# Reordering one network block inside a woven single-core kernel: the u sigmoids before the z sigmoids, the scan one step earlier, an idle step between two top-1 units

## The reference: four blocks, of which the last two are touched

```python
def scan_block(hidden):                       # L1_attn
    x, z = split(hidden @ in_proj_w.T, 2)     # 256 + 256 features
    xc = silu(depthwise_conv4(x) + conv_b); u = xc
    dt_low, Bp, Cp = split(u @ x_proj_w.T, [8, 24])
    delta = softplus(dt_low @ dt_proj_w.T + 2 * dt_proj_b)
    # 16 states n: s = exp(delta * A[n]) * s + delta * Bp[n] * u ;  y += s * Cp[n]
    y = (y + u * D) * silu(z)
    return y @ out_proj_w.T
x = layernorm(x + scan_block(x))

def top1_block(x):                            # L1_ffn
    probs = softmax(x @ wg); idx = argmax(probs)
    # a token keeps its expert if fewer than T/8 earlier tokens chose it
    return gate * (x @ W[idx].T + b[idx])
x = layernorm(x + top1_block(x))
```

## Time and profile before

| | us |
|---|---|
| median of 3 runs | 1405.06 |
| lowest, highest | 1401.98, 1413.62 |
| the profiled execution's own time | 1411.83 |
| its span | 1410.0 |
| busy: PE, DVE, ACT, POOL | 905.6, 972.0, 594.3, 84.2 |
| mean granted TensorE clock (share of full) | 0.776 |

### The profile page before, as it was taken

One profiled execution on the slowest core, in us unless ns is written; L12 is line 12 of the kernel. 1 busy time (PEld: TensorE's weight loads), 2 busy tenths in 40 slices (PEclk: granted clock), 3 DMA queues, 4 the chain that ended last, 5 costly groups with the idle time before them and its releaser, 6 DMA issues.

```text
span 1410.0 us, 29222 instructions
## 1 busy us (share of the span) xinstructions
PE 905.6 (64%) x11808; PEld 545.3 (39%) x11808; DVE 972.0 (69%) x2254; ACT 594.3 (42%) x1299; POOL 84.2 (6%) x56
## 2 busy tenths in 40 slices
PE   4655656777567577788566677777657566472554
PEld 2444535444334244445234244444334244240122
DVE  5345543655689987656699987655689987335985
ACT  3333332466633332476633332466643331445320
POOL 0000000011000000020000000011000000030630
PEclk8556858599758889697768889698658789676897
DMA  4110110311223210311223210211223310302420
GB/s 143 31 40 10 33 39 10 66 35 39 67 68 87 69 31 18 67 36 37 67 68 87 69 31 12 57 42 39 66 63 86 76 31 10 68 1 62 112 67 8
DMA packets 84822, 72.19 MB, mean 51 GB/s; under 512 B 24528, under 2 KB 63440, under 8 KB 84496
## 3 DMA queue, kind: packets, MB, share of 16 engines
q1 hardware_dynamic: 84688, 70.34, 19.7%
HBM read 66.51 MB, written 3.80 MB: 50 GB/s over the span
## 4 chain that ended last, share of the span: by engine, by line
DVE 33%; PE 20%; ACT 12%; issue 11%; DMA 3%; SPq 2%; DVEq 0%; POOL 0%; ACTq 0%; POOLq 0%
DVE SG L1727 5%; PE bank L716 3%; PE bank L543 2%; DVE Y L1820 2%; DVE XP L1740 2%; PE bank L874 2%; DVE CV L1740 2%; SPq L480 2%; ACT QBD L1063 2%; DVE bank L1727 1%; PE bank L748 1%; PE bank L824 1%; ACT relu_s L1027 1%; DVE big L1715 1%; DVE big L1702 1%
## 5 line engine op out<-in xcount | busy, mean ns | idle before, releaser
L716 PE MATMUL bank<-onehot,tparts 128*32 128x256 bf16 x3840 | 134.8, 300 | 45.3 <-DVE onehot L1506 41.6
L716 PEld LDWEIGHTS bank<-onehot,tparts 128*32 128x32 bf16 x3840 | 108.7, 105 | 80.3 <-issue 70.7
L874 PE MATMUL bank<-XP,CO 128*128 128x512 f32 x128 | 86.1, 809 | 60.6 <-DVE XP L1738 33.2
L1727 DVE TENSOR_TENSOR_SCAN SG<-big 128x512 f32<-128x512 f32 x96 | 111.7, 1205 | 0.9
L1215 ACT ACTIVATE big<-DEL,Aneg 128x512 f32<-128x512 f32 x96 | 63.8, 715 | 102.5 <-DVE SG L1727 96.7
L1027 ACT ACTIVATE relu_s<-bank,nml 128x192 f32<-128x192 f32 (+1 forms) x128 | 52.9, 426 | 112.0 <-DVE nml L1472 112.0
L874 PE MATMUL bank<-CV,CO 128*128 128x512 f32 x128 | 77.3, 735 | 32.4 <-DVE CV L1740 20.4
L1467 DVE TENSOR_REDUCE ml<-bank 128x2 f32<-128x384 f32 (+1 forms) x64 | 33.8, 569 | 71.1 <-PE bank L651 38.5
L1506 DVE TENSOR_SCALAR onehot<-ib,CO 128x1024 bf16<-128x1024 f16 x160 | 69.5, 477 | 15.7 <-PE bank L716 14.5
L748 PE MATMUL bank<-GT,QBD 128*32 128x32 f32 x3072 | 56.6, 208 | 34.9 <-DVE G L1515 22.1
L543 PE MATMUL bank<-CO,relu_s 128*128 128x128 f32 (+2 forms) x256 | 45.8, 339 | 44.7 <-ACT relu_s L1027 44.7
(11 more groups left out here) (306 smaller groups left out, 2002.7 us busy)
## 6 DMA issues: line engine op xcount, KB each, us to landing
BC<-bc_rows SPq DMA_DIRECT2D x128, 256.0 KB, 4.4
ib<-idx_rows SPq DMA_DIRECT2D x64, 256.0 KB, 4.1
big<-comb_rows SPq DMA_DIRECT2D x8, 1024.0 KB, 10.0
rows_bounce<-RO SPq DMA_DIRECT2D x256, 8.5 KB
W<-w SPq DMA_DIRECT2D x1, 2818.0 KB, 14.8
RB<-rows_bounce SPq DMA_DIRECT2D x16, 136.0 KB, 2.1
X<-x SPq DMA_DIRECT2D x4, 256.0 KB, 3.0
out<-CV SPq DMA_DIRECT2D x4, 256.0 KB, 2.3
```

Source lines behind the costliest of these rows:

```text
L716: m = mm(bank[2 + c % 2][32 * bb:32 * bb + 32, 256 * kind:256 * kind + 256], tparts[:, kt, part, 32 * kind:32 * kind + 32], onehot[:, n % ...
L874: mm(bank[5 + j][:, :], ident, hC[(n - 1) % 2][:, j, :], start=(n == 1), stop=(n == DS)).then_inc(ysum.sem, ysum.up())
L1727: m = dve.tensor_tensor_scan(state, decay, dBu[:, n % 2, j, :], 0.0, ALU.mult, ALU.add)
```

## The change

ACT and DVE: the two u sigmoids (and `U` times the conv's result) come before the two z sigmoids (and `SZ` times z). PE, ACT, DVE, SP and POOL: `SCAN_IN_PHASES` is 9 instead of 10, so that everything from the u projection to the second top-1 unit lies one step earlier. `TOP1_PHASES` is 9 instead of 8, with an idle step between the second and the third top-1 unit, so the third and fourth unit and the last norm stay in their steps. No instruction is added, removed or resized.

```diff
@@ PE @@
                     mm(bank[3 + k][:, :], w("inp")[:, k * P:(k + 1) * P], XRT[:, :], start=True, stop=True).then_inc(xz_ps.sem, xz_ps.up())
-                for _ in range(3):
+                for _ in range(2):
                     yield
                 pe.wait_ge(u_ok.sem, u_ok.at(b, 2))
...
                 top1_out(1)
+                yield
                 yield
                 pe.wait_ge(e_used.sem, e_used.at(b, 2))
@@ ACT @@
                 yield
+                for j in range(2):
+                    act.wait_ge(cv_ok.sem, cv_ok.at(b, j + 1))
+                    sigmoid(CV[:, j, :], eu[:, j, :], U[:, j, :], ue_ok)
+                yield
                 for k in range(2):
                     act.wait_ge(xz_ps.sem, xz_ps.at(b, k + 3))
                     sigmoid(bank[5 + k][:, :], ez[:, k, :], SZ[:, k, :], ze_ok)
-                yield
-                for j in range(2):
-                    act.wait_ge(cv_ok.sem, cv_ok.at(b, j + 1))
-                    sigmoid(CV[:, j, :], eu[:, j, :], U[:, j, :], ue_ok)
-                yield
                 yield
                 act.wait_ge(xd_ps.sem, xd_ps.at(b, 1))
...
-                for i in range(NT):
-                    if i == NT - 1:
-                        norm_scale(b, 4)
-                    yield
+                for _ in range(NT):
+                    yield
+                norm_scale(b, 4)
+                yield
                 yield
@@ DVE @@
                 for j in range(2):
-                    dve.wait_ge(ze_ok.sem, ze_ok.at(b, j + 1))
-                    TT(SZ[:, j, :], SZ[:, j, :], bank[5 + j][:, :], ALU.mult).then_inc(sz_ok.sem, sz_ok.up())
-                yield
-                for j in range(2):
                     dve.wait_ge(ue_ok.sem, ue_ok.at(b, j + 1))
                     TT(U[:, j, :], U[:, j, :], CV[:, j, :], ALU.mult).then_inc(u_ok.sem, u_ok.up())
                     dve.wait_ge(u_ok.sem, u_ok.now(b))
+                yield
+                for j in range(2):
+                    dve.wait_ge(ze_ok.sem, ze_ok.at(b, j + 1))
+                    TT(SZ[:, j, :], SZ[:, j, :], bank[5 + j][:, :], ALU.mult).then_inc(sz_ok.sem, sz_ok.up())
                 for _ in range(3):
                     yield
-                yield
                 dve.wait_ge(dt_sp.sem, dt_sp.at(b, 1))
...
+                    if i == 1:
+                        yield
                     if i == NT - 1:
                         norm_sums(b, Y2)
@@ constants @@
-ROUTE_PHASES, EXPERT_PHASES, NORM_PHASES, SCAN_IN_PHASES, SCAN_OUT_PHASES, TOP1_PHASES = 2, 18, 2, 10, 3, 8
+ROUTE_PHASES, EXPERT_PHASES, NORM_PHASES, SCAN_IN_PHASES, SCAN_OUT_PHASES, TOP1_PHASES = 2, 18, 2, 9, 3, 9
```

More of the change, by code:

```diff
@@ L1180, in rest @@
                 yield
-                for k in range(2):
-                    act.wait_ge(xz_ps.sem, xz_ps.at(b, k + 3))
-                    sigmoid(bank[5 + k][:, :], ez[:, k, :], SZ[:, k, :], ze_ok)
-                yield
                 for j in range(2):
@@ L1188, in rest @@
                 yield
+                for k in range(2):
+                    act.wait_ge(xz_ps.sem, xz_ps.at(b, k + 3))
+                    sigmoid(bank[5 + k][:, :], ez[:, k, :], SZ[:, k, :], ze_ok)
                 yield
```

## The result

The changed kernel took **1412.53 us** (median of 20 runs, 1404.32 to 1423.27) against 1405.60 us for the kernel before beside it (20 runs, 1401.46 to 1413.62). The ratio on record is 1.004, 95% interval 1.0021 to 1.0058, which makes it some 5.6 us slower (3 to 8); the two medians themselves lie 6.9 us apart. A second measurement, on another occasion, gave 1.0032 (1.0011 to 1.0053). The forecast was +3.9 us, and within 1%.

A forecast was written before the change was run, and what follows sets the result against it. It took DVE's full middle to bound the woven rows, leaving their two ends to matter, and the lone rest as a chain; +7.2 - 3.3 = +3.9 us on 1411.8 gave 1415.7, median set at 1409.0, range 1397 to 1419.

The forecast's parts named there:

- +2.4 us per woven row: Both ends of each woven row together: picked scores at 542.6 instead of 538.45, partly regained; +7.2 us over three rows.
- Lone rest: After the last conv: z's sigmoids run beside the u projection, so `XD` starts at 1282.7 instead of 1286.02; -3.3 us.
- The bound that I had given: Lone rest: gain of 0 if PE waited for the z product, done at 1283.4.
- Term A: Start end of a woven row: one DVE wait of 8.1 us, none for `RB`, work done at 398.4, not 398.05; +0.4 us.
- The norm's sums end at about 519.9, as they did: Back end of a woven row: the earlier norm gains nothing, since DVE waits 2.4 us for PE's last sum.
- Pick 0 at full clock: Back end of a woven row: pick 0 starts at 526.7 behind the router logits and takes 2.8 us.
- rival 1: Back end of woven rows: clock falls for pick 0, 2.7 us more each, 8.1 in three, 1417 in all; chance 0.20.
- My own signs: Wrong if pick 0 came ahead of 526 us; right if tile 3's picked scores started about 4 us later against the norm's sums.
- the rule: Skill's statement that idle stretches between matmul bursts bring the array to half clock; by it pick 0 would be slow.
- the single gap at which I had pointed: Ahead of pick 0 in the woven rows: PE without work for 3.2 of 3.8 us.
- the row from which I argued: Profile row where, after a 3.07 us gap, 48 pick matmuls took 2.75 us, as long as 96 at full clock.

The follow-up runs named there:

- xrt_first: The changed kernel with the last tile's `QBD` copies one step later on ACT, behind the copy of `XRT`; ratio 0.9987 to the kernel before.
- swap_only: The kernel before with u's sigmoids and products ahead of z's in every row, scan and idle step not moved; ratio 0.9962 to the kernel before.
- lone_only: The kernel before with u ahead of z in the lone rest alone, woven rows as they were; ratio 0.9959 to the kernel before.
- fill_gap: The changed kernel plus 16 unused PE transposes ahead of the router logits in the woven rows; ratio 0.9963 to the kernel before.
- xrt_first_fill: The changed kernel with `XRT` copied ahead of `QBD` and 16 unused transposes ahead of the router logits; ratio 0.9962 to the kernel before.
- fill_four: The changed kernel plus 4 unused PE transposes ahead of the router logits; ratio 0.9998 to the kernel before.

## Why the prediction was right, and where it was right by luck

**The sum.** Forecast +2.4 us per woven row and -3.3 in the lone rest, +3.9. By the table the changed kernel has +2.4 and +3.2 us per row and -3.5 in the lone rest: +3.7 and +6.1, and the ratios say +5.6 and +4.5. The agreement is one of means: the three rows of the first profile are +2.7, +4.2 and +0.1.

**Lone rest: right.** The step of ACT's z sigmoids beside the projection is there, and the lone rest is 3.5 us shorter on average (forecast 3.3). The bound that I had given, PE waiting for z's product, came about as well, but cost only some 0.2 us, since `XD` ended just before it.

**Term A, +0.4: too high by 1.1 us.** The mechanism was right line by line: one wait, no wait for `RB`, the same `XD`. But rotation, merge and the part of the polynomial up to L1701 are done at 391.2 us, which with 6.15 added is 397.3, where they were at 398.05: -0.7. What I mis-sized was dt's matmuls, for which I took the 2.82 us of the earlier trace rows. In their new place they took 1.95 us, in the second row too, where they took 3.46 us before. PE of the changed kernel, and the windows around these matmuls, first of the changed kernel (clock 1.00), then of the kernel before (0.69):

```profile
365.39 1.95 PE L865 MATMUL bank<-XD,W 8*128 8x512 f32 x4 [0.77 <-ACT XD L1191]
```

```profile
365.30:367.30 2.00, 1.91 (x8) 0.70 (x10) 1.49 (x7) 0.25 (x1) 0.00 (x0) 1.00 0.17 41
```

```profile
374.10:376.90 2.80, 2.80 (x9) 0.77 (x6) 1.01 (x4) 0.39 (x1) 0.00 (x0) 0.69 0.33 110
```

The remaining 0.2 us is unexplained.

**Term A in the sum: not there.** I wrote that the +2.4 us per row has the 0.4 of term A inside. It hasn't: the norm's sums were set at 519.9 as before, and +2.4 is what the back end adds from there (560.1 against 557.70).

**"The norm's sums end at about 519.9, as they did": wrong.** They ended at 511.26, which with 6.15 added is 517.4, 2.4 us sooner than in the kernel before. DVE waited 0.82 us for PE's last sum instead of the 2.4 I had given; with that wait I had filled the place of the query's turn, which the shift puts behind the sums.

**Pick 0 at full clock: wrong.** This is rival 1, to which I gave 0.20. It happened in every row of both profiles of the changed kernel. I priced it at 2.7 us; filling the gap gave back 3.4 us per row. From the norm's sums behind the scan to those of the last norm the forecast had +2.4 us, and against the earlier trace rows it was +5.2 in the first row (37.84 to 43.02). The 2.8 us between them are, to 0.1 us, the router logits (1.87 instead of 1.06 us) and pick 0 (4.87 instead of 2.80).

**Two errors met.** The early norm and the slow pick cancel: with the 6.15 us of this row added, the picked scores start at 542.9 (forecast 542.6) and the last norm's sums end at 560.4 (forecast 560.1). That the total came out is luck to that extent. Such agreement to 0.3 us proved nothing about the steps between; only the traces and the experiments showed which were true. My own signs had caught it: I had named a pick 0 ahead of 526 us as a sign of being wrong, and it starts at 525.1; and the picked scores start 6.9 us later against the norm's sums, not about 4.

**What I said of the rule.** The traces show slow matmuls behind a wait of 2.66 us, with the clock at 0.83 in the 20 us from the norm's sums on. The Trainium skill, TensorE: Matmul & The Clock Gate, "HAM oscillation — how this bites in real kernels", says that idle stretches between bursts bring the array back to half clock; the fall inside PE's wait in the changed kernel agrees with it. But the single gap at which I had pointed doesn't decide, as xrt_first shows. Nor did the row from which I argued. The same 48 matmuls behind the same 3.07 us took 1.73, 2.75 and 2.75 us in the three woven rows of the kernel before, and 1.49, 1.68 and 2.75 in those of the changed one:

```profile
360.37 1.73 PE L716 MATMUL bank<-onehot,tparts 128*32 128x256 bf16 x48 [3.07 <-DVE onehot L1506]
```

I had picked one of three. What in PE's work does decide stays open: no run varied it alone.

**The faster versions.** swap_only, lone_only, fill_gap and xrt_first_fill all stand at 0.996 to before, 5 us or so faster than it and 10 us faster than the change. They can't be told apart. The simplest is the swap alone, and no arrangement with the shift was faster than the swap alone.

## What to carry to other kernels

Moving a woven block by one step changes the order at both its ends: price the wait that each end's neighbours had been covering, and look at whether the idle step lands where an engine was waiting for another anyway. Before believing a forecast that PE keeps its speed, ask what its activity would be ahead of the burst, and test it with a few matmuls that nobody reads: that is the cheapest way to separate "late" from "slow". Don't subtract two whole profiles where untouched stretches differ by more than the effect; compare stretches between landmarks, over all rows, and take the spread from two kernels whose code in that stretch is the same. And when a row is used as evidence that a gap costs clock, read every place where that gap occurs.

## What the runs showed of the hardware that I had not expected

Sixteen transposes without a use, 3.66 us with the four real ones, gave 10 us in 1410. The granted clock of the 20 us from the norm's sums on rose with them from 0.83 to between 0.91 and 1.00. The clock can fall within a burst, with no wait in between: in fill_four the router logits ran at full speed (1.06 us), and the 96 picks right behind them took 4.47 us instead of 2.80. And the same instructions in the same order ran at either level in two kernels: pick 0 in the old order, behind 1.44 us of waiting, took 2.80 us in the kernel before and 4.39 us in the first row of lone_only.
